# Moving two groups' query and key projections around the first maxima of an attention block

## The reference

```python
mod = (_silu(L0_c) @ L0_wmod).reshape(L0_c.shape[0], 6, 1, -1)
sa, ca, ga, sb, cb, gb = (mod[:, 0], mod[:, 1], mod[:, 2], mod[:, 3], mod[:, 4], mod[:, 5])
...
h = _layernorm(x, axis=-1) * (1 + ca) + sa
x = x + ga * _L0_attn_ref(h, ...)      # softmax(q k^T / 4) v, then a projection
h = _layernorm(x, axis=-1) * (1 + cb) + sb
x = x + gb * _L0_ffn_ref(h, ...)       # base matmul + one of 8 adapters per 256 tokens' losses
```

## Time and profile before

| | us |
|---|---|
| median of 3 runs | 1007.9 |
| lowest and highest | 1005.11, 1008.78 |
| the profiled execution | 1006.01 |
| its span in the trace | 1004.2 |
| TensorE busy | 962.7 |
| VectorE busy | 813.2 |
| ScalarE busy | 661.7 |

### The profile page before, as it was taken

One profiled execution on the slowest core, in us unless ns is written; L12 is line 12 of the kernel. 1 busy time (PEld: TensorE's weight loads), 2 busy tenths in 40 slices (PEclk: granted clock), 3 DMA queues, 4 the chain that ended last, 5 costly groups with the idle time before them and its releaser, 6 DMA issues.

```text
span 1004.2 us, 16485 instructions
## 1 busy us (share of the span) xinstructions
PE 962.7 (96%) x5794; PEld 480.8 (48%) x5794; DVE 813.2 (81%) x1657; ACT 661.7 (66%) x1295; POOL 284.4 (28%) x391
## 2 busy tenths in 40 slices
PE   6989999999899999999999999999999999999998
PEld 5444344343344445554454454545454455644476
DVE  4789989899688887788888888788778788889455
ACT  2148787887577777667668786766657767666831
POOL 4210133022155241200336431300237413116320
PEclk9879999999899999999999999999999999999999
DMA  6850051242550513242223511404424311132001
GB/s 180 141 92 23 12 107 45 56 95 71 80 96 12 96 34 66 44 85 81 70 87 60 85 44 45 75 13 78 130 70 80 58 29 35 38 96 77 29 6 48
DMA packets 47890, 66.93 MB, mean 67 GB/s; under 512 B 12139, under 2 KB 32112, under 8 KB 47796
## 3 DMA queue, kind: packets, MB, share of 16 engines
q1 hardware_dynamic: 46572, 65.00, 29.9%
q0 software_dynamic: 384, 0.79, 0.5%
q10 hardware_dynamic: 852, 0.09, 0.1%
HBM read 27.48 MB, written 12.59 MB: 40 GB/s over the span
## 4 chain that ended last, share of the span: by engine, by line
PE 77%; DVE 9%; ACT 5%; issue 2%; POOL 2%; DMA 2%; SPq 1%; ACTq 0%; DVEq 0%; POOLq 0%
PE pE L811 25%; PE pO L811 22%; PE pX L811 18%; PE pM L811 11%; DVE mx L1293 4%; ACT P L1118 2%; DMA QO<-lo 1%; ACT h1T L1159 1%; DVE h2f L1454 1%; ACT h2f L1205 1%; ACT hi L1175 1%; DVE lo L1374 1%; SPq L1867 0%; DVE junk L1430 0%; DMA P<-in_wmod 0%
## 5 line engine op out<-in xcount | busy, mean ns | idle before, releaser
L1293 DVE TENSOR_REDUCE mx<-pM 128x1 f32<-128x512 f32 x1006 | 629.7, 682 | 76.7 <-PE pM L811 71.4
L1118 ACT ACTIVATE P<-pE 128x512 f32<-128x512 f32 x996 | 526.7, 601 | 181.1 <-PE pE L811 177.8
L811 PE MATMUL pM<-KO,QO 48*128 48x512 f32 x1006 | 370.7, 455 | 6.8 <-DMA QO<-lo 3.3
L811 PE MATMUL pE<-QO,KO 50*128 50x512 f32 x996 | 349.2, 438 | 11.9 <-ACT h1T L1159 5.1
L811 PEld LDWEIGHTS pE<-QO,KO 50*128 50x128 f32 x996 | 164.9, 187 | 234.1 <-issue 125.1
L811 PE MATMUL pO<-P,V 128*17 128x512 f32 x2048 | 257.9, 598 | 5.1 <-ACT P L1118 5.1
L811 PEld LDWEIGHTS pM<-KO,QO 48*128 48x128 f32 x1006 | 164.3, 187 | 41.3 <-DVE mx L1293 28.8
L811 PEld LDWEIGHTS pO<-P,V 128*17 128x17 f32 x2048 | 40.5, 96 | 103.2 <-issue 88.1
L1695 POOL CAST mh<-mxc 128x16 fp32r<-128x16 f32 x32 | 6.5, 203 | 285.7 <-DVE mxc L1302 285.5
L811 PE MATMUL pX<-h1T,wqkv_s 128*128 128x512 f32 x112 | 59.2, 642 | 1.9 <-DVE lo L1374 1.5
L1754 POOL TENSOR_TENSOR Hs<-h2f,Hs 128x512 fp32r<-128x512 f32 x28 | 35.7, 1284 | 83.6 <-ACT Hs L1235 68.3
(11 more groups left out here) (301 smaller groups left out, 1023.4 us busy)
## 6 DMA issues: line engine op xcount, KB each, us to landing
outs<-osb SPq DMA_DIRECT2D x31, 256.0 KB, 2.9
KO<-hi SPq DMA_DIRECT2D x56, 128.0 KB, 4.0
QO<-hi SPq DMA_DIRECT2D x56, 128.0 KB, 5.1
x<-in_x SPq DMA_DIRECT2D x20, 256.0 KB, 3.6
out<-x SPq DMA_DIRECT2D x16, 256.0 KB, 2.1
AT<-outs SPq DMA_DIRECT2D x15, 256.0 KB
asum<-wsum SPq DMA_DIRECT2D x15, 256.0 KB
KO<-lo SPq DMA_DIRECT2D x28, 128.0 KB, 3.6
```

What stands on the lines that cost most here:

```text
L811: return e.matmul(o, lhsT, rhs, start=start, stop=stop)
L1118: e.activation(P[:, u % 3, j, :], bank(s), ACT.Exp).then_inc(*empties(s))
L1293: e.tensor_reduce(mx[:, hq % 2, k:k + 1, kh], bank(s), AX.X, ALU.max, negate=True).then_inc(*empties(s))
```

## The change

Group 1's four qk pieces are taken out of the lead and set ahead of the first maximum. Group 2's two qk steps are taken out of the lead as well; they are the first longer work that waits when the scores begin, so that they come as single pieces after bursts without a PV step, and group 2's copies follow when they are done. The steps left in the lead (setupc, two modmm, four V) come after each six maxima instead of each four. Group 1's copies and the five loads stand behind setupc in the list.

```diff
+    out += [(("qk", 0, 1, half), p) for half in range(2) for p in range(2)]
+
-    beside = deque([("qk", 0, 1, 0), ("qk", 0, 1, 1), ("setupc",), ("modmm", 1), ("modmm", 2)])
-    beside += [("v", 0, t) for t in range(4)] + [("qk", 0, 2, 0), ("qk", 0, 2, 1)]
+    beside = deque([("setupc",), ("modmm", 1), ("modmm", 2)] + [("v", 0, t) for t in range(4)])
     for i in range(LEAD):
-        if i and i % 4 == 0 and beside:
+        if i and i % 6 == 0 and beside:
             s = beside.popleft()
             out += [(s, p) for p in range(PIECES[s[0]])] if s[0] in PIECES else [s]
-            if s == ("qk", 0, 1, 1):
+            if s == ("setupc",):
                 out += copies(1) + [("loads",)]
...
-    moving.extend(copies(2))
+    waiting["long"] = [("qk", 0, 2, half) for half in range(2)]
```

## The result

The changed kernel takes 1011.1 us in the median of 20 runs (1006.91 to 1016.97), against 1007.66 (1004.9 to 1011.82) of the kernel before beside it: a ratio of 1.0038, interval 1.0023 to 1.0052. It is slower by 0.4%, where 0.4% faster was forecast, and 3 us above the range. The profiled execution took 1011.13, with a span of 1009.3.

What follows compares the result with a forecast made beforehand. TensorE was taken as the bound (busy 962.7 of 1004.2 us), with losses in the first 90 us; -5.75 + 0.9 + 0.9 = -3.95 took the profiled 1006.0 to 1002.1, or the median 1007.9 to 1003.9; range 1001 to 1008.

Steps and rivals of the forecast that it cites:

- Term: 0.7 us. At the landing as it is this is the value I take: In the lead, modmm 1 waits 1.0 us for wmod's load, landing after 7.9 us; cost to VectorE 0.7 us.
- the lead is held up: Rival: wmod lands 2 us later, or TensorE drops to half clock at modmm 1; +2 us, 1005.9; chance 0.14.
- the prediction's own signs of being wrong: Half clock in the lead, VectorE waiting there over 2 us, or the 4 us there at 90 us and gone at the end.
- 0.9 for lo: First scores: group 2's two lo steps on VectorE, 1.5 us, partly absorbed; cost 0.9 us, bounds 0.3 and 1.5.
- 0.9 for the pieces: First scores: group 2's pieces one and two at half clock, 1.9 us each instead of 0.95; cost 0.9, bounds 0 and 1.9.
- VectorE's stock hides half of it: First scores: VectorE's stock covers half the extra time of group 2's pieces one and two at half clock, leaving 0.9 us.
- what was moved comes back: Rival: group 2's four pieces (3.8) and both lo steps (1.5) lie bare among the scores; -0.4 us, no change; chance 0.09.
- the first reduction at 28.13 against 28.85: Start of the lead: with group 1's pieces ahead of M0, VectorE's first reduction starts at 28.85, 1.2 us later than before.
- the shift beyond the tenth group: Behind the tenth score group the written order is unchanged, so the shift, some 4 us earlier, should stand to the end.
- a step after four maxima sets the pace of the lead: Lead before: both engines have the same period, V steps 2.59 us apart on TensorE, four reductions 2.4 us on VectorE.
- The lead was forecast to shrink from 37.5 to 29.8 us: VectorE's lead at one step per six maxima: 48 x 0.60 plus small terms, 29.8 us; before it took 37.5.
- -5.75 for the lead as forecast: End of the lead: M47 reduced at 59.35 against 65.1, a gain of 5.75 us, the 0.7 load wait included.

Runs made afterwards that it cites:

- e1_gate: The changed kernel, with SP waiting for wmod's second part to land before issuing group 1's copies: 1008.92 us, ratio 1.0008 to the kernel before.
- f4_g2_lead5: The changed kernel with group 2's steps back in the lead, one step per five maxima, wmod load left behind setupb: 1013.06 us, ratio 1.0048.
- e2_early: The changed kernel with the load of wmod's second part issued in the opening, right behind wdT: 1004.32 us, ratio 0.9974 to the kernel before.
- h1_lo_later_early: e2_early with VectorE's two lo steps of group 2 put three reductions later: 1003.29 us (7 runs), ratio 0.9978 to the kernel before.
- h2_lead4_again: e2_early with group 2 back in the lead and one step per four maxima, the repeat run: 1003.87 us, ratio 0.9967 to the kernel before.

## Why the prediction was wrong

**The step that failed** is "Term: 0.7 us. At the landing as it is this is the value I take", the load of wmod. It was sized with a landing of 7.9 us and with modmm 1 at full clock. VectorE's idle time there is 6.68 + 0.73 = 7.4 us in place of 0.7. The error of 6.7 has three parts, by the runs. The landing became 12.3 us, since group 1's copies are issued 1.4 us behind the load instead of 9.2: 3.5 us in modmm 1's start against the gated load (39.34 and 35.84). The clock fell in the wait: 3.57 - 1.88 = 1.7. The rest, some 1.5, is that even with the gated load modmm 1 starts at 35.84 and not at 35.15 (0.7), and that the first wait of 0.73, at setupc, was not in the sum: the clock was at half there, where the sum had it full. Gating bought back only 1.8 at the first mark, as VectorE then waited 1.54 elsewhere in the lead; issuing the load early bought back 6.9.

I had this case as the rival "the lead is held up" with a chance of 0.14. Its two causes, the later load and half clock at modmm 1, I priced as one or the other, at 2 us; they came together. In all three kernels in which modmm 1 waited for the load (after, e1_gate, f4_g2_lead5) it ran at half clock, and in e2_early, which had no wait, at full. Two of the prediction's own signs of being wrong were there: half clock in the lead, from 30.0 to 33.4 and from 36.8 to 43.6, and a wait of VectorE over 2 us. The rule cited from the Trainium skill, "DMA: Bandwidth & Descriptors", section "Issuing engines are not separate DMA queues", agrees with the trace: 7.9 us became 12.3 with the copies beside it (10.9 in f4_g2_lead5) and 8.9 without. It stood in the text and did not enter the sum.

**The second mis-sized term** is what the scores give back, 0.9 for lo and 0.9 for the pieces: 1.8 in place of 5.8, or 4.6 in e2_early. Both bounds of lo were right (the steps lie bare, 1.4), but the chain was missing from the sum: a piece on TensorE at half clock (2.07), then hi on ScalarE, then lo on VectorE, which can't go on with its reductions while it waits 1.74 for hi, and TensorE then lacks banks and VectorE maxima (1.85, 1.56). "VectorE's stock hides half of it" was wrong. h1_lo_later_early puts some 1.7 us on the order of the lo steps, as counted above; how the rest divides between the clock and the pieces themselves stays open, since the filling changed more than the clock. The rival "what was moved comes back" had this case with all of it bare at 5.3 us, and a chance of 0.09: for the scores it was the nearest, and since the load had used up the gain of the lead, both rivals came at once.

**What was right.** Group 1's pieces at full clock; the first reduction at 28.13 against 28.85; no gap of VectorE in the lead behind the load; the gates and rows of the maxima without a wait; the spell of half clock behind the lead (64.1 to 77.8, longer than the 10.2 us before); the shift beyond the tenth group stands to the end, but for the steps at the tenth and eleventh marks, which sum to 1.1 us. With the load out of the way M47 is done at 58.8, where 59.35 was forecast.

**Right for a reason that did not matter:** that a step after four maxima sets the pace of the lead. In h2_lead4_again VectorE has hardly a gap with that spacing. The lead was forecast to shrink from 37.5 to 29.8 us, by 7.7. In the kernel before, VectorE's two waits for hi (2.41 and the 1.95 of the line at 58.91) and four lo steps of 0.67 make 7.0 of this; the period of four maxima and a step is left with 0.6 or so. The number was right because all six left the lead with their pieces, which the prediction didn't list.

The sum with the measured terms: -5.75 for the lead as forecast, -0.7 for the earlier first reduction, +6.7 for the load, +0.3 for small differences, which makes the +0.5 measured for M47; then +5.8 for the scores. That is +6.3 at M80, and +5.0 at the end, where the spans differ by 5.1. The medians differ by 3.4.

## What to carry to other kernels

When a step is moved forward, check every load that it needs by "issued plus landing" with the transfers that will then run beside it, not with the landing of the old trace; and price the wait with the slower clock behind it: here each wait for the load had it. A step that passes over three engines in turn costs, where banks are short, the waits between them and not the sum of its instructions. And take apart a change of several parts: here the one part that pays (group 1 ahead of the first maximum) was worth a third of a per cent with the load moved, while one that came with it, group 2 among the scores, left the kernel before 2.8 us later at the third mark.

## What was not expected of the hardware

- A load of 1 MB landed 7.9 us after its issue with the next copy 9.2 us behind it, 8.9 with group 1's copies held back until it had landed, 9.3 to 11.9 behind two loads of 0.5 MB (nine kernels), and 12.3 and 10.9 with copies of 128 KB issued 1.4 and 1.3 us behind it. As one and the same place gives 9.3 to 11.9, a landing read from one trace is good to a microsecond or two, and so is the part of the 12.3 that is put down to the copies. The copies waited too: 9.0 us to landing, against 4.2 gated.
- A wait of 2.04 us was as bad for the following four matmuls as one of 4.79: 3.57 us in both. In e1_gate the clock fell at 34.3, half a microsecond into the wait.
- The clock fell at setupc in the kernel after (30.0) and in e2_early (29.3), where TensorE's longest waits since 26 us were 0.63 and 0.58 us. In h1_lo_later_early, with the same order up to there, it stayed full (1.00 over 18 to 58 us). The prediction had seen it fall only in waits of 3.33 and 1.72 us.
- Extra matmuls that keep the clock full (1.00 in both windows above) made the kernel slower, as the score and the maximum of a pair, which take 0.60 us together, took 0.98 with one between them.
- Runs of one and the same kernel, the one before, differ with the mean granted clock: executions at 0.988 take about 1006.0 us, at 0.985 about 1008.3, at 0.981 about 1011.2. That is the 7 us from lowest to highest, and the reason why differences of 2 us show in the first marks and not in the medians.
